# Two GRU recurrences on one core: recurrent products written several times, shorter input chunks, another order on VectorE

## The chip, the core and the metric

The kernel runs on one core of one Trainium2 chip. The metric is the time of one execution on the device, in microseconds. The core's engines run side by side and meet at semaphores: TensorE (PE in the rows; PEld is its weight load), VectorE (DVE), ScalarE (ACT), GpSimd (POOL) and SyncE (SP).

## The reference

Four layers are applied to an input of 8 images of 16 x 16 positions with 96 channels: a Fourier layer, a Toeplitz layer, and two GRU layers (L2 and L3). The GRU layers take most of the time. Each runs four GRUs over the 256 positions (two weight sets, each forward and reversed), and one step of a GRU is

```
def step(hprev, gxt):
    gh = hprev @ whh.T + bhh
    r = jax.nn.sigmoid(gxt[:, :h] + gh[:, :h])
    z = jax.nn.sigmoid(gxt[:, h:2 * h] + gh[:, h:2 * h])
    n = jnp.tanh(gxt[:, 2 * h:] + r * gh[:, 2 * h:])
    hn = (1.0 - z) * n + z * hprev
    return (hn, hn)
```

with h = 96, a batch of 8 and gx the input's share, known for all steps beforehand. There are 256 such steps in a layer, one after the other, so 512 in the kernel.

## The kernel before

Each GRU layer has an input part (`gru_input`), the steps (`gru_steps`) and an output part (`gru_output`). The change is in `gru_steps` alone.

The four GRUs stand in two **groups** of two (g = 0 and 1; the two inside a group are j = 0 and 1, so a group works on 16 columns, PER). The groups don't depend on each other, and each engine takes them in turn, so that one group's products run while the other group's gates are computed.

To keep fp32 accuracy from fp16 products, the state is held as a sum of two fp16 parts, `h_hi` and `h_lo`, and each weight as two as well. For each step and group TensorE runs (L1123, in `add`) twelve products with h_hi (three gates, two GRUs, two weight parts), waits for h_lo, and runs six products with h_lo. Each has 8 columns. The gates come in the order candidate, reset, keep; after the last h_lo product of the reset gate `reset_summed` is raised, after the last of all `keep_summed`. Then come some **input products** (L1105): the input's share is not computed step by step but for a chunk of STEPS = 8 steps, 36 products of 64 columns for the next chunk, dealt out over the steps of the current one.

All sums stand in PSUM, in two banks a group and chunk parity: `early` (reset, and the candidate's two summands) and `late` (keep). A bank holds 512 columns, of which `early` uses 384 and `late` 128.

ScalarE, for each group: sigmoid of the reset sum (L1071), sigmoids of the keep sum for z and 1-z (L1073, L1074), tanh of the candidate (L1077). VectorE: `candidate`, a scan that makes r times the recurrent share plus the input share (L1022); `kept_part`, z times the old state (L1029); `new_state`, two scans that make the same new state, once rounded to fp16 as h_hi (L1037, first, since TensorE waits for it) and once in fp32 into `states` (L1039); `rest`, which subtracts h_hi from the state and gives h_lo (L1045). `candidate` waits for the reset gate; `rest` waits for the fp32 state; `new_state` waits for tanh and for `kept_part`.

Each engine works strictly in the order written. On VectorE this is

```
for q in range(SEQ):
    candidate(0, q)
    rest(1, q - 1)
    kept_part(0, q)
    new_state(0, q)
    rest(0, q)
    candidate(1, q)
    kept_part(1, q)
    new_state(1, q)
```

Of the kernel before, what the change touches and what calls it, by code (L numbers as in the profile page):

```python
# [25 lines left out]
F32 = mybir.dt.float32  # L26
# [4 lines left out]
P = 128  # L31
BATCH, SIDE, C = 8, 16, 96
# [28 lines left out]
GRUS = ("f_%s_fw", "b_%s_rv", "f_%s_rv", "b_%s_fw")  # L61
GATES = 3

STEPS = 8
CHUNK_COUNT = SEQ // STEPS
GROUPS = 2

AFTER_0 = 0.7
PER = 2 * BATCH


def flat(ap):

    return ap.rearrange("p a b -> p (a b)")
# [893 lines left out]
def gru_steps(nc, layer, weights, forward, backward, states):  # L968
# [3 lines left out]
    with ExitStack() as ctx:  # L972
# [9 lines left out]

        h_hi = pairs("h_hi", [C + 1, 2, PER, 2], F16)
        h_lo = pairs("h_lo", [C, 2, PER], F16)
        early = [[ctx.enter_context(nc.psum_tensor(f"{layer}s_early{g}{p}", [P, 4, PER, STEPS], F32)) for p in range(2)] for g in range(GROUPS)]
        late = [[ctx.enter_context(nc.psum_tensor(f"{layer}s_late{g}{p}", [P, 4, PER, STEPS], F32)) for p in range(2)] for g in range(GROUPS)]
        reset_sum = lambda g, p: early[g][p][:, 0]
        cand_sum = lambda g, p: early[g][p][:, 1:3].rearrange("p a c s -> p (a c) s").rearrange("p (c k) s -> p c k s", k=2)
        keep_sum = lambda g, p: late[g][p][:, 0]
        warm = sb("warm", [C, 1])  # L990
        prepared = sem("prepared")

# [5 lines left out]
        with nc.Block() as block:  # L998

            @block.vector  # L1000
            def _(e):

                e.memset(warm[:], 0.0).then_inc(prepared, 1)
                for g in range(GROUPS):
                    for buffer in (reset[g], renew[g], terms[g], h_lo[g]):
                        e.memset(buffer[:], 0.0).then_inc(prepared, 1)
                    e.memset(states[g][:, 0], 0.0).then_inc(prepared, 1)
                    e.memset(h_hi[g][0:C], 0.0).then_inc(prepared, 1)
                    e.memset(h_hi[g][C:C + 1], 1.0).then_inc(prepared, 1)
                e.wait_ge(prepared, PREPARED)  # L1010

                for s, n in ((updated[1], 2), (hi_ready[0], 1), (hi_ready[1], 1), (lo_ready[0], 1)):
                    e.sem_inc(s, n)

                BEFORE = (0, 2)

                def candidate(g, q):

                    p, s = q // STEPS % 2, q % STEPS
                    x = q % 2  # L1020
                    e.wait_ge(activated[g], 3 * q + 1)
                    e.tensor_tensor_scan(flat(cand[g][:, x]), flat(reset[g][:, x]), flat(cand_sum(g, p)[0:C, :, :, s]), 0.0,  # L1022
                                         ALU.mult, ALU.add).then_inc(cand_ready[g], 1)

                def kept_part(g, q):

                    x = q % 2
                    e.wait_ge(activated[g], 3 * q + 2)
                    e.tensor_tensor(terms[g][:, x, :, 1], keep[g][:, x], states[g][:, q, :, 1], ALU.mult)\  # L1029
                        .then_inc(updated[g], 1)  # L1030

                def new_state(g, q):

                    x = q % 2
                    e.wait_ge(activated[g], 3 * q + 3)
                    e.wait_ge(updated[g], 2 * q + 1 + BEFORE[g])
                    e.tensor_tensor_scan(flat(h_hi[g][0:C, x]), flat(renew[g][:, x]), flat(terms[g][:, x]), 0.0,  # L1037
                                         ALU.mult, ALU.add).then_inc(hi_ready[g], 1)
                    e.tensor_tensor_scan(flat(states[g][:, q + 1]), flat(renew[g][:, x]), flat(terms[g][:, x]), 0.0,  # L1039
                                         ALU.mult, ALU.add).then_inc(updated[g], 1)  # L1040

                def rest(g, q):

                    e.wait_ge(updated[g], 2 * q + 2 + BEFORE[g])
                    e.tensor_tensor(h_lo[g][:, q % 2], states[g][:, q + 1, :, 1], h_hi[g][0:C, q % 2, :, 1],  # L1045
                                    ALU.subtract).then_inc(lo_ready[g], 1)

                for q in range(SEQ):
                    candidate(0, q)
                    rest(1, q - 1)  # L1050
                    kept_part(0, q)
                    new_state(0, q)
                    rest(0, q)
                    candidate(1, q)
                    kept_part(1, q)
                    new_state(1, q)
                e.wait_ge(updated[1], 2 * SEQ + BEFORE[1])

            @block.scalar
            def _(e):  # L1060
# [4 lines left out]
                for q in range(SEQ):  # L1065
                    p, s = q // STEPS % 2, q % STEPS
                    x = q % 2
# [11 lines left out]
            @block.tensor  # L1079
            def _(e):  # L1080
                def inputs(p, chunk):

                    out = []
                    cols = slice(chunk * STEPS, (chunk + 1) * STEPS)
                    for gru in range(len(GRUS)):
                        g, j = divmod(gru, 2)
                        source = forward if gru < 2 else backward
                        mine = slice(j * BATCH, (j + 1) * BATCH)

                        def share(dst, gate, first):  # L1090
                            for wp, xp in ((0, 0), (1, 0), (0, 1)):
                                rows = C if xp else C + 1
                                lhsT = weights.input[0:rows, wp, GATES * gru + gate, :]
                                rhs = source[0:rows, xp, :, cols]
                                out.append((dst, lhsT, rhs, first and (wp, xp) == (0, 0)))


                        share(reset_sum(g, p)[:, mine], 0, j == 0)
                        share(cand_sum(g, p)[:, mine, 1], 2, False)
                        share(keep_sum(g, p)[:, mine], 1, j == 0)  # L1100
                    return out

                def run(product):
                    dst, lhsT, rhs, start = product
                    return e.matmul(dst, lhsT, rhs, start=start, stop=False, skip_group_check=True)  # L1105

                for product in inputs(0, 0):
                    run(product)
                e.wait_ge(prepared, PREPARED)
                for q in range(SEQ):  # L1110
                    p, s = q // STEPS % 2, q % STEPS
                    x = (q + 1) % 2
                    if s == 0:
                        following = q // STEPS + 1
                        ahead = inputs(1 - p, following) if following < CHUNK_COUNT else []
                        sent = 0
                    for g in range(GROUPS):
                        def add(gate, wp, xp, j):
                            mine = slice(j * BATCH, (j + 1) * BATCH)
                            rows = C if xp else C + 1  # L1120
                            rhs = h_lo[g][:, x, mine] if xp else h_hi[g][:, x, mine, 1]
                            dst = (reset_sum(g, p)[:, mine, s], keep_sum(g, p)[:, mine, s], cand_sum(g, p)[:, mine, 0, s])[gate]
                            return e.matmul(dst, weights.hidden[0:rows, wp, GATES * (2 * g + j) + gate, :], rhs,  # L1123
                                            start=False, stop=False, skip_group_check=True)


                        e.wait_ge(hi_ready[g], q + 1)
                        for gate in (2, 0, 1):
                            for j in range(2):
                                add(gate, 0, 0, j)  # L1130
                                add(gate, 1, 0, j)

                        e.wait_ge(lo_ready[g], q + 1)
                        for gate in (2, 0, 1):
                            for j in range(2):
                                last = add(gate, 0, 1, j)
                            if gate == 0:
                                last.then_inc(reset_summed[g], 1)
                        last.then_inc(keep_summed[g], 1)

                        due = round((s + (AFTER_0 if g == 0 else 1)) * len(ahead) / STEPS)
                        for product in ahead[sent:due]:
                            run(product)
                        sent = due
# [196 lines left out]
```

## Time and profile before

| | |
|---|---|
| median of 3 runs | 1243.77 us (1241.73 to 1247.79) |
| profiled execution, its own time | 1242.83 us |
| its span in the trace | 1241.1 us |
| TensorE busy | 1066.6 us, 86% |
| VectorE busy | 931.8 us, 75% |
| ScalarE busy | 665.8 us, 54% |
| mean granted TensorE clock | 0.585 of full speed |

The two recurrences run from about 298 to 733 us and from about 780 to 1216 us. Busy shares are averages over stages with different limits; a recurrence is bound by a chain of small operations that wait for each other, so it has to be read from the timeline of single steps: start times, one after the other, on all engines. TensorE's clock has two levels, 1.2 and 2.4 GHz; the rows give it as a share of 2.4 GHz.

### The profile page before, as it was taken

The page shows a single profiled execution, that of the slowest core. Times are in us where ns is not written, and L with a number is a line of the kernel's source. Part 1 is how long each engine was busy: PE and PEld are TensorE (multiplying, and loading weights), DVE is VectorE, ACT ScalarE, POOL GpSimd, SP SyncE. Part 2 cuts the span into 40 slices and gives each one's busy share as a digit, 9 for nine tenths or more (in the row PEclk, how much of TensorE's full clock was granted, in tenths as well). Part 3 has the DMA queues.
Part 4 walks back from the last instruction along what each step waited for, and adds up shares of the span by engine and source line. Part 5 has one row for each costly group of instructions (what it writes and reads, how often), then busy time and mean ns, then how long its engine had stood idle before and what let it go on. Part 6 is the DMA issues. An engine that isn't in the chain of part 4 may idle for free. (4 is left out here: it accounts for less than half of the span.)

```text
span 1241.1 us, 56119 instructions
## 1 busy us (share of the span) xinstructions
PE 1066.6 (86%) x22390; PEld 814.7 (66%) x22390; DVE 931.8 (75%) x5703; ACT 665.8 (54%) x4269; POOL 116.7 (9%) x96
## 2 busy tenths in 40 slices
PE   3778799768999999999999968899999999999985
PEld 2555254355777777777777755677777777777775
DVE  3553799984777777777777785677777777777776
ACT  4224620007666666666666654666666666666663
POOL 1001389910000000000000001000000000000000
PEclk9587899957555555555555557655555555555555
DMA  4000500000000000000000000000000000000000
GB/s 117 2 8 5 129 1 1 1 5 2 4 4 3 4 4 4 3 4 4 4 4 3 4 2 5 3 4 4 4 4 3 4 4 4 3 4 4 4 3 27
DMA packets 8225, 12.63 MB, mean 10 GB/s; under 512 B 5745, under 2 KB 7121, under 8 KB 7674
## 3 DMA queue, kind: packets, MB, share of 16 engines
q1 hardware_dynamic: 7962, 9.05, 2.9%
q8 instruction: 175, 2.87, 1.0%
q14 instruction: 88, 0.72, 0.2%
HBM read 8.26 MB, written 0.79 MB: 7 GB/s over the span
## 5 line engine op out<-in xcount | busy, mean ns | idle before, releaser
L1123 PE MATMUL L3s_early<-L3s_h_hi,L_w_hidden 97*128 97x8 f16 x4096 | 195.3, 177 | 38.7 <-DVE L3s_h_hi L1037 5.2
L1123 PE MATMUL L2s_early<-L2s_h_hi,L_w_hidden 97*128 97x8 f16 x4096 | 195.3, 177 | 37.8 <-DVE L2s_h_hi L1037 5.4
L1123 PEld LDWEIGHTS L3s_early<-L3s_h_hi,L_w_hidden 97*128 97x128 f16 x4096 | 148.8, 105 | 111.2 <-DVE L3s_h_hi L1037 81.8
L1123 PEld LDWEIGHTS L2s_early<-L2s_h_hi,L_w_hidden 97*128 97x128 f16 x4096 | 148.8, 105 | 110.0 <-DVE L2s_h_hi L1037 77.4
L1037 DVE TENSOR_TENSOR_SCAN L3s_h_hi<-L3s_renew,L3s_terms 96x32 f16<-96x32 f32 x512 | 113.2, 221 | 84.8 <-ACT L3s_terms L1077 59.1
L1037 DVE TENSOR_TENSOR_SCAN L2s_h_hi<-L2s_renew,L2s_terms 96x32 f16<-96x32 f32 x512 | 113.2, 221 | 83.8 <-ACT L2s_terms L1077 57.4
L1077 ACT ACTIVATE L3s_terms<-L3s_cand 96x16 f32<-96x16 f32 x512 | 111.5, 218 | 106.0 <-DVE L3s_cand L1022 105.9
L1077 ACT ACTIVATE L2s_terms<-L2s_cand 96x16 f32<-96x16 f32 x512 | 111.5, 218 | 104.7 <-DVE L2s_cand L1022 104.6
L1123 PE MATMUL L3s_early<-L3s_h_lo,L_w_hidden 96*128 96x8 f16 x2048 | 131.0, 174 | 0.2 <-DVE L3s_h_lo L1045 0.2
L1123 PE MATMUL L2s_early<-L2s_h_lo,L_w_hidden 96*128 96x8 f16 x2048 | 130.9, 174 | 0.2 <-DVE L2s_h_lo L1045 0.2
L1123 PE MATMUL L2s_late<-L2s_h_hi,L_w_hidden 97*128 97x8 f16 x2048 | 130.0, 174 | 0.0
L1123 PE MATMUL L3s_late<-L3s_h_hi,L_w_hidden 97*128 97x8 f16 x2048 | 130.0, 174 | 0.0
L1071 ACT ACTIVATE L2s_reset<-L2s_early 96x16 f32<-96x16 f32 x512 | 93.0, 182 | 55.1 <-PE L2s_early L1123 55.1
L1071 ACT ACTIVATE L3s_reset<-L3s_early 96x16 f32<-96x16 f32 x512 | 93.0, 182 | 54.7 <-PE L3s_early L1123 54.7
L693 DVE SCALAR_TENSOR_TENSOR l_acc<-l_v,coef,l_acc 96x384 f32<-96x384 f32 (+11 forms) x88 | 103.6, 1241 | 0.4
L1022 DVE TENSOR_TENSOR_SCAN L3s_cand<-L3s_reset,L3s_early 96x32 f32<-96x32 f32 x512 | 102.5, 200 | 1.2 <-ACT L3s_reset L1071 1.2
L1022 DVE TENSOR_TENSOR_SCAN L2s_cand<-L2s_reset,L2s_early 96x32 f32<-96x32 f32 x512 | 102.3, 200 | 1.2 <-ACT L2s_reset L1071 1.2
L1123 PE MATMUL L2s_late<-L2s_h_lo,L_w_hidden 96*128 96x8 f16 x1024 | 102.7, 174 | 0.0
L1123 PE MATMUL L3s_late<-L3s_h_lo,L_w_hidden 96*128 96x8 f16 x1024 | 102.7, 174 | 0.0
L1039 DVE TENSOR_TENSOR_SCAN L_states<-L2s_renew,L2s_terms 96x32 f32<-96x32 f32 x512 | 99.9, 195 | 0.0
L1039 DVE TENSOR_TENSOR_SCAN L_states<-L3s_renew,L3s_terms 96x32 f32<-96x32 f32 x512 | 99.9, 195 | 0.0
L1045 DVE TENSOR_TENSOR L2s_h_lo<-L_states,L2s_h_hi 96x16 f16<-96x16 f32 x512 | 87.9, 172 | 9.1
(243 smaller groups left out, 2477.7 us busy)
## 6 DMA issues: line engine op xcount, KB each, us to landing
L_wih_raw<-in_L_wih SPq DMA_DIRECT2D x2, 1152.0 KB, 11.0
l_w_raw<-in_L_w SPq DMA_DIRECT2D x1, 1296.0 KB
L_w_hidden_raw<-in_L_whh SPq DMA_DIRECT2D x2, 576.0 KB
stream<-in_x SPq DMA_DIRECT2D x2, 384.0 KB, 3.8
out<-stream SPq DMA_DIRECT2D x4, 192.0 KB, 2.1
l_idft<-in_idft SPq DMA_DIRECT2D x1, 400.0 KB
rpe_lw<-in_rpe_lw SPq DMA_DIRECT2D x1, 384.0 KB
l_dft<-in_dft SPq DMA_DIRECT2D x1, 288.0 KB, 2.9
```

Of the source, the lines that this page charges most:

```text
L693: e.scalar_tensor_tensor(out=row(to, acc), in0=row(of, v), scalar=coef[:, m, axis, at:at + 1], in1=row(to, acc), op0=ALU.mult, op1=ALU.add ...
L1022: e.tensor_tensor_scan(flat(cand[g][:, x]), flat(reset[g][:, x]), flat(cand_sum(g, p)[0:C, :, :, s]), 0.0, ALU.mult, ALU.add).then_inc(can ...
L1037: e.tensor_tensor_scan(flat(h_hi[g][0:C, x]), flat(renew[g][:, x]), flat(terms[g][:, x]), 0.0, ALU.mult, ALU.add).then_inc(hi_ready[g], 1)
L1039: e.tensor_tensor_scan(flat(states[g][:, q + 1]), flat(renew[g][:, x]), flat(terms[g][:, x]), 0.0, ALU.mult, ALU.add).then_inc(updated[g], 1)
L1045: e.tensor_tensor(h_lo[g][:, q % 2], states[g][:, q + 1, :, 1], h_hi[g][0:C, q % 2, :, 1], ALU.subtract).then_inc(lo_ready[g], 1)
L1071: e.activation(reset[g][:, x, :, 1], reset_sum(g, p)[0:C, :, s], ACT.Sigmoid).then_inc(activated[g], 1)
L1077: e.activation(terms[g][:, x, :, 0], cand[g][:, x, :, 1], ACT.Tanh).then_inc(activated[g], 1)
L1123: return e.matmul(dst, weights.hidden[0:rows, wp, GATES * (2 * g + j) + gate, :], rhs, start=False, stop=False, skip_group_check=True)
```

## The change

1. Each recurrent product is written to three places (reset) or four (candidate, keep) in one matmul: the same 8 columns of the state are read three or four times (a broadcast of the moving operand), and the output goes to the 8 columns that are read later and to 16 or 24 columns of the same bank that nobody reads. A recurrent matmul so has 24 or 32 columns instead of 8.
2. To make room for these, a chunk has 4 steps instead of 8: the banks are laid out as eight parts of 16 x 4 columns in place of four parts of 16 x 8. The input products become 36 of 32 columns for every 4 steps.
3. On VectorE the second group's candidate scan stands ahead of the first group's `rest`.

```
-STEPS = 8
+STEPS = 4
...
-        early = [[... psum_tensor(f"{layer}s_early{g}{p}", [P, 4, PER, STEPS], F32) ...
-        late = [[... psum_tensor(f"{layer}s_late{g}{p}", [P, 4, PER, STEPS], F32) ...
+        early = [[... psum_tensor(f"{layer}s_early{g}{p}", [P, 8, PER, STEPS], F32) ...
+        late = [[... psum_tensor(f"{layer}s_late{g}{p}", [P, 8, PER, STEPS], F32) ...
...
                     new_state(0, q)
+                    candidate(1, q)
                     rest(0, q)
-                    candidate(1, q)
                     kept_part(1, q)
...
-                            dst = (reset_sum(g, p)[:, mine, s], keep_sum(g, p)[:, mine, s], cand_sum(g, p)[:, mine, 0, s])[gate]
-                            return e.matmul(dst, weights.hidden[0:rows, wp, GATES * (2 * g + j) + gate, :], rhs,
+                            halves = early[g][p].rearrange("p a (c k) s -> p a c k s", k=2)
+                            spread = (early[g][p][:, 0:7:3, mine, s], late[g][p][:, 0:4, mine, s],
+                                      halves[:, (slice(1, 8, 2), slice(2, 6))[j], :, 0, s])[gate]
+                            copies = spread.shape[1]
+                            return e.matmul(spread, weights.hidden[0:rows, wp, GATES * (2 * g + j) + gate, :],
+                                            rhs.unsqueeze(1).to_broadcast([rows, copies, BATCH]),
```

On VectorE, in the middle of the first recurrence's steps, the digit behind a name being the group (behind `early` the group and the chunk's parity). Before:

```order
L1037 SCALAR_TENSOR_TENSOR L2s_h_hi0<-L2s_renew0,L2s_terms0 96x32
L1039 SCALAR_TENSOR_TENSOR L2_states0<-L2s_renew0,L2s_terms0 96x32
L1045 TENSOR_TENSOR L2s_h_lo0<-L2_states0,L2s_h_hi0 96x16
L1022 SCALAR_TENSOR_TENSOR L2s_cand1<-L2s_reset1,L2s_early10 96x32
L1029 TENSOR_TENSOR L2s_terms1<-L2s_keep1,L2_states1 96x16
L1037 SCALAR_TENSOR_TENSOR L2s_h_hi1<-L2s_renew1,L2s_terms1 96x32
L1039 SCALAR_TENSOR_TENSOR L2_states1<-L2s_renew1,L2s_terms1 96x32
L1022 SCALAR_TENSOR_TENSOR L2s_cand0<-L2s_reset0,L2s_early00 96x32
L1045 TENSOR_TENSOR L2s_h_lo1<-L2_states1,L2s_h_hi1 96x16
```

And after, where all lines of the file are one higher here:

```order
L1038 SCALAR_TENSOR_TENSOR L2s_h_hi0<-L2s_renew0,L2s_terms0 96x32
L1040 SCALAR_TENSOR_TENSOR L2_states0<-L2s_renew0,L2s_terms0 96x32
L1023 SCALAR_TENSOR_TENSOR L2s_cand1<-L2s_reset1,L2s_early10 96x32
L1046 TENSOR_TENSOR L2s_h_lo0<-L2_states0,L2s_h_hi0 96x16
L1030 TENSOR_TENSOR L2s_terms1<-L2s_keep1,L2_states1 96x16
L1038 SCALAR_TENSOR_TENSOR L2s_h_hi1<-L2s_renew1,L2s_terms1 96x32
L1040 SCALAR_TENSOR_TENSOR L2_states1<-L2s_renew1,L2s_terms1 96x32
L1023 SCALAR_TENSOR_TENSOR L2s_cand0<-L2s_reset0,L2s_early00 96x32
L1046 TENSOR_TENSOR L2s_h_lo1<-L2_states1,L2s_h_hi1 96x16
```

Group 0's h_lo has gone behind group 1's candidate scan, as group 1's h_lo stood behind group 0's already. On TensorE, for one group and the turn after it, before (the last figure is partitions x columns, `x8` the number of such matmuls in a row):

```order
L1123 MATMUL L2s_early<-L2s_h_hi,L_w_hidden 128x8 x8
L1123 MATMUL L2s_late<-L2s_h_hi,L_w_hidden 128x8 x4
L1123 MATMUL L2s_early<-L2s_h_lo,L_w_hidden 128x8 x4
L1123 MATMUL L2s_late<-L2s_h_lo,L_w_hidden 128x8 x2
L1105 MATMUL L2s_late<-L_backward,L_w_input 128x64
```

And after, where the recurrent products are at L1127 and the input products at L1106:

```order
L1127 MATMUL L2s_early<-L2s_h_hi,L_w_hidden 128x4x8 x2
L1127 MATMUL L2s_early<-L2s_h_hi,L_w_hidden 128x32 x2
L1127 MATMUL L2s_early<-L2s_h_hi,L_w_hidden 128x3x8 x4
L1127 MATMUL L2s_late<-L2s_h_hi,L_w_hidden 128x4x8 x4
L1127 MATMUL L2s_early<-L2s_h_lo,L_w_hidden 128x4x8
L1127 MATMUL L2s_early<-L2s_h_lo,L_w_hidden 128x32
L1127 MATMUL L2s_early<-L2s_h_lo,L_w_hidden 128x3x8 x2
L1127 MATMUL L2s_late<-L2s_h_lo,L_w_hidden 128x4x8 x2
L1106 MATMUL L2s_late<-L_backward,L_w_input 128x32 x3
```

The number and order of the recurrent products are the same, each is three or four times as wide; the input products of a turn are six behind group 0 and three behind group 1, of 32 columns.

## Rows read from the trace of the kernel before

**Rows 1.** The page: busy time, and the granted clock in 40 slices.

```profile
PE 1066.6 (86%) x22390; PEld 814.7 (66%) x22390; DVE 931.8 (75%) x5703; ACT 665.8 (54%) x4269; POOL 116.7 (9%) x96
...
PEclk9587899957555555555555557655555555555555
```

**Rows 2.** Groups of instructions from 784 to 1200 us: count, busy us, mean ns.

```profile
L1123 PE MATMUL L3s_late<-L3s_h_lo,L_w_hidden 96*128 96x8 f16 x978 | 98.1, 174 | 0.0
L1022 DVE TENSOR_TENSOR_SCAN L3s_cand<-L3s_reset,L3s_early 96x32 f32<-96x32 f32 x489 | 97.9, 200 | 0.0
```

**Rows 3.** Timeline of one step at 1.2 GHz: start us, us, engine, line.

```profile
784.33 0.32 PE L1105 MATMUL L3s_early<-L_forward,L_w_input 97*128 97x64 f16 x3
...
785.24 0.22 DVE L1037 TENSOR_TENSOR_SCAN L3s_h_hi<-L3s_renew,L3s_terms 96x32 f16<-96x32 f32 x1
...
785.41 0.18 ACT L1071 ACTIVATE L3s_reset<-L3s_early 96x16 f32<-96x16 f32 x1 [0.21 <-PE L3s_early L1123]
...
785.52 0.38 PE L1123 MATMUL L3s_early<-L3s_h_hi,L_w_hidden 97*128 97x8 f16 x8
...
785.61 0.17 DVE L1045 TENSOR_TENSOR L3s_h_lo<-L_states,L3s_h_hi 96x16 f16<-96x16 f32 x1
785.70 0.21 DVE L1022 TENSOR_TENSOR_SCAN L3s_cand<-L3s_reset,L3s_early 96x32 f32<-96x32 f32 x1
...
785.86 0.25 PE L1123 MATMUL L3s_early<-L3s_h_lo,L_w_hidden 96*128 96x8 f16 x4
...
785.95 0.22 ACT L1077 ACTIVATE L3s_terms<-L3s_cand 96x16 f32<-96x16 f32 x1 [0.20 <-DVE L3s_cand L1022]
...
786.15 0.18 ACT L1071 ACTIVATE L3s_reset<-L3s_early 96x16 f32<-96x16 f32 x1
786.19 0.22 DVE L1037 TENSOR_TENSOR_SCAN L3s_h_hi<-L3s_renew,L3s_terms 96x32 f16<-96x32 f32 x1 [0.22 <-ACT L3s_terms L1077]
...
786.34 0.20 DVE L1039 TENSOR_TENSOR_SCAN L_states<-L3s_renew,L3s_terms 96x32 f32<-96x32 f32 x1
786.45 0.19 DVE L1022 TENSOR_TENSOR_SCAN L3s_cand<-L3s_reset,L3s_early 96x32 f32<-96x32 f32 x1
...
786.67 0.22 ACT L1077 ACTIVATE L3s_terms<-L3s_cand 96x16 f32<-96x16 f32 x1 [0.20 <-DVE L3s_cand L1022]
...
786.93 0.22 DVE L1037 TENSOR_TENSOR_SCAN L3s_h_hi<-L3s_renew,L3s_terms 96x32 f16<-96x32 f32 x1
```

**Rows 4.** Timeline, the second recurrence's first steps.

```profile
781.15 0.18 ACT L1071 ACTIVATE L3s_reset<-L3s_early 96x16 f32<-96x16 f32 x1 [0.53 <-PE L3s_early L1123]
...
781.36 0.22 DVE L1022 TENSOR_TENSOR_SCAN L3s_cand<-L3s_reset,L3s_early 96x32 f32<-96x32 f32 x1 [1.16 <-ACT L3s_reset L1071]
781.50 0.15 DVE L1045 TENSOR_TENSOR L3s_h_lo<-L_states,L3s_h_hi 96x16 f16<-96x16 f32 x1
...
781.70 0.26 PE L1123 MATMUL L3s_early<-L3s_h_lo,L_w_hidden 96*128 96x8 f16 x4 [0.21 <-DVE L3s_h_lo L1045]
...
782.00 0.18 ACT L1071 ACTIVATE L3s_reset<-L3s_early 96x16 f32<-96x16 f32 x1 [0.17 <-PE L3s_early L1123]
...
782.14 0.36 PE L1123 MATMUL L3s_early<-L3s_h_hi,L_w_hidden 97*128 97x8 f16 x8
...
783.83 0.38 PE L1123 MATMUL L3s_early<-L3s_h_hi,L_w_hidden 97*128 97x8 f16 x8
```

**Rows 5.** Stretches: length, TensorE's busy us, further engines' in the second, granted clock.

```profile
741.00:754.00 13.00, 13.00 (x63) 0.50 0.00 1
...
782.00:784.00 2.00, 1.70 (x49) 1.39 (x48) 1.61 (x13) 1.35 (x11) 0.00 (x0) 0.90 0.00 0
```

**Rows 6.** Groups from 400 to 700 us: single input products.

```profile
L1105 PE MATMUL L2s_late<-L_backward,L_w_input 96*128 96x64 f16 x44 | 9.4, 214 | 0.0
```

**Rows 7.** Timeline, the first recurrence's first step.

```profile
298.94 0.22 DVE L1022 TENSOR_TENSOR_SCAN L2s_cand<-L2s_reset,L2s_early 96x32 f32<-96x32 f32 x1 [1.16 <-ACT L2s_reset L1071]
...
299.59 0.18 ACT L1071 ACTIVATE L2s_reset<-L2s_early 96x16 f32<-96x16 f32 x1 [0.18 <-PE L2s_early L1123]
```

More of the change, by code:

```diff
@@ L984, in gru_steps @@
         h_lo = pairs("h_lo", [C, 2, PER], F16)
-        early = [[ctx.enter_context(nc.psum_tensor(f"{layer}s_early{g}{p}", [P, 4, PER, STEPS], F32)) for p in range(2)] for g in range(GROUPS)]
-        late = [[ctx.enter_context(nc.psum_tensor(f"{layer}s_late{g}{p}", [P, 4, PER, STEPS], F32)) for p in range(2)] for g in range(GROUPS)]
+        early = [[ctx.enter_context(nc.psum_tensor(f"{layer}s_early{g}{p}", [P, 8, PER, STEPS], F32)) for p in range(2)] for g in range(GROUPS)]
+        late = [[ctx.enter_context(nc.psum_tensor(f"{layer}s_late{g}{p}", [P, 8, PER, STEPS], F32)) for p in range(2)] for g in range(GROUPS)]
         reset_sum = lambda g, p: early[g][p][:, 0]
```

## Prediction

> **What bounds the kernel now.** The page first [rows 1]: the span is 1241.1 us, TensorE (PE) is busy 86% of it, VectorE (DVE) 75%, and its costliest lines are the recurrent products and the small operations of the GRU step. Then the clock line of the slices [rows 1]: in nearly all slices of the two recurrences TensorE is granted half its speed, 1.2 GHz. The invitation is to blame the clock. The table of groups [rows 2] gives the size of the stage: 489 candidate scans in 416 us, two to a step, are 1.70 us a step, and 512 steps in all are about 871 us of the span.
>
> What ends each step is read from the timeline of one step at 1.2 GHz [rows 3], by start times. The first group's h_hi scan (L1037) starts at 785.24, the state scan (L1039) right behind it (0.15 us, as at 786.34); the difference h_lo (L1045), which needs that scan's result, at 785.61; only then the second group's candidate scan (L1022) at 785.70, although its reset gate (L1071) had started at 785.41 and ended at 785.59; its tanh at 785.95; its h_hi scan at 786.19; its state scan at 786.34; the first group's candidate scan at 786.45; the tanh at 786.67; and the first group's next h_hi scan at 786.93. That is a closed ring of VectorE and ScalarE (ACT) alone: 0.37+0.09+0.25+0.24+0.15+0.11+0.22+0.26 = 1.69 us, the whole period. No matmul is in it. TensorE's part runs beside it with a little room. The path of one group alone is h_hi scan to h_hi product 785.24 to 785.52 (0.28), product to reset gate 785.52 to 786.15 (0.63), reset gate to candidate scan 0.21 where nothing stands between (781.15 to 781.36 [rows 4]), to tanh 0.22, to scan 0.26: 1.60 us.
>
> The same step at 2.4 GHz stands in the first steps of the second recurrence. The first group's h_hi products start at 782.14 and 783.83 [rows 4], again 1.69 us apart, though the clock is still 0.90 on average from 782 to 784 [rows 5], so 1.00 for all but the last 0.4 us. So **a fast TensorE by itself buys nothing in today's order**: the ring does not contain it.
>
> **The change, part by part.**
>
> *Wider products.* Each step's 36 recurrent matmuls stream 24 columns (reset) or 32 (candidate, keep) instead of 8. Two prices: the spacing, and the last column's arrival. Spacing: twelve h_hi matmuls at 1.2 GHz take 785.52 to 785.86, 28 ns each [rows 3]; three of 64 columns take 0.32 us (784.33) where one takes 0.21 [rows 3, 6], so 55 ns each. 32 columns lie halfway in columns, but 64 columns at 1.2 GHz are 53 ns, so 32 are 27 ns and fit under the 28 ns that a small product takes anyway. I take zero; the other end, the 64-column price, adds 27 ns to each of three gaps ahead of the reset sum. Arrival: a product of 64 columns lasts 214 ns, of 8 columns 174 [rows 2, 6], 40 ns for 56 columns, so 16 more columns in the last reset product cost 11 ns. At 2.4 GHz I take half, 6 ns (an estimate from the two clock levels). The Trainium skill (TensorE: Matmul & The Clock Gate, Single matmul latency) prices columns at N/1.2 and N/2.4 ns, 13 and 7 ns here; the trace agrees within its modelled ends.
>
> *The clock.* What could be gained from it is small: the half ring below is 0.85 us at one level and 0.86 at the other. In the steps the h_hi and h_lo products start 0.34 us apart (785.52 and 785.86 [rows 3]), TensorE never rests long, and the clock is 0.50 all the same. Will it rise? TensorE was granted 1.2 GHz for the whole 13 us in which it ran 96-column fp32 products (L1217) back to back, busy 13.00 of 13.00 us [rows 5]; and it fell from 2.4 to 1.2 GHz some 3 us after the second recurrence began its steps [rows 5], though the products run there as densely as they ever do. The high slices lie where products of hundreds of columns run densely [rows 1]. The widened step is 36 products of 24 or 32 columns and 9 of 32, with waits between; that is nearer to the rows where it stayed low or fell. I take 1.2 GHz. The Trainium skill (same page, Why this matters for your kernels) says that the clock stays high as long as TensorE has no long idle gaps between bursts; by that rule it would be high in the steps already and the wider products could change nothing. The trace does not follow the rule here.
>
> *Chunks of four.* The input products become 36 of 32 columns per four steps: nine a step instead of 4.5, 9 x 28 ns against 4.5 x 55: nothing. They stand behind the reset and keep products in TensorE's queue. First group: six each step, 0.17 us, second: three. A group's turn on TensorE is then 0.34 us for the h_hi products (785.52 to 785.86), six h_lo products, 0.17, and six input products, 0.17: 0.68 us of the 0.87 that a half step has, so 0.19 us are idle and cover them. If h_lo comes 0.1 us late that cover still holds; without it each 0.1 us would be 0.1 on the half step. The first chunk's products lie ahead of step 0, beside the memsets.
>
> *The second candidate scan ahead of the first group's low half.* This breaks the present ring: state scan to candidate scan directly, 0.11 instead of 0.23+0.09, so that ring would be 1.48 us (786.34 to 786.45 for the direct link [rows 3]). But it closes another. The order on VectorE is then candidate(0), h_lo(1), ..., candidate(1), h_lo(0): each group's h_lo stands behind the other group's candidate scan, the h_lo products wait for it, the reset gate waits for these, and the group's own candidate scan waits for the reset gate. Half of the ring is: candidate scan, h_lo, h_lo product, reset gate, next candidate scan. It is in the trace twice where the scan had waited, as it will in the new order, at the first step of each recurrence: 781.36 to 781.50 (0.14), to the product at 781.70 (0.20), to the reset gate at 782.00 (0.30), and from gate to scan 781.15 to 781.36 (0.21) [rows 4]: **0.85 us** at 2.4 GHz. In the other recurrence scan to reset gate is 298.94 to 299.59 (0.65) [rows 7], with 0.21 **0.86 us**; I take that for 1.2 GHz. Both halves must pass within one step, so the period is 2 x 0.86 = 1.72 us before the columns. Add 11 ns to each: 2 x 0.871 = 1.742 us. Today's order has only one such half in a ring; the other passes through tanh and the scans, 1.60 us in all.
>
> **The sum.** At 1.2 GHz: 1.742 - 1.69 = +0.052 us a step, x 512 = +26.6 us. The profiled execution took 1242.83 us (0.9 below the median of 1243.77, which I leave aside), so **1269 us**. Everything outside the recurrences stays: a higher clock in the steps is not counted on for the output products, which come after a pause of several us.
>
> **Rivals.**
>
> *The clock rises (all or much of the time).* For it: more than three times the columns, and the fp32 products' columns may not compare with fp16's. Then each half is 0.85+0.006, the period 1.712, +0.022 x 512 = +11: **1254 us**. Alternating levels lie between. Chance 0.22.
>
> *Faster.* The two sampled halves are first steps. If the new order lets VectorE and TensorE run as smoothly as now, each link takes its shortest row: VectorE to its next operation 0.11 (786.34 to 786.45), h_lo to product 0.20, product to reset gate 0.29 (785.86 to 786.15), gate to scan 0.21 [rows 3, 4], 0.81 us, so 1.62 to 1.64, with columns at 2.4 GHz 1.65: -0.04 x 512 = -20, **1222 us**. The deciding point is a half of 0.845 us; under it the reorder gains, and at 0.80 the single group's path (1.60) takes over at 1242.8 - 46 = 1197. Against it: in both samples the product waits for h_lo, which adds the weight load to the path. Chance 0.27.
>
> *Wide patterns cost as 64 columns.* Three gaps ahead of the reset sum cost 27 ns more each in each half: 2 x 0.08 x 512 = +83 on the forecast, 1350. A quarter of that is 1290. The arithmetic above speaks against it. Chance 0.07.
>
> *Nothing moves*: the loss by the new ring and the gain by its shorter links meet. 1238 to 1249. Chance 0.10, in part beside the edges of the two others.
>
> **How the numbers follow.** Forecast 0.34 with its own range 1258 to 1282; risen clock 0.22; faster 0.27; dear columns 0.07; nothing 0.10. The range goes to 1222 below (half of the faster case is left out) and 1284 above. Changes under 0.5%, or 6 us, cannot be told from none by a measurement. Faster by over 0.5% (under 1237.6) is the faster case, 0.27; within 0.5% the last case and the risen clock's lower edge, 0.14; slower the rest, 0.59.
>
> **What would show it.** The step length by the starts of one group's h_hi products: 1.74 us, or 1.71 or 1.65. VectorE's candidate scan should follow the state scan after a wait on the reset gate and no more on h_lo, and TensorE should wait on h_lo (L1046) at each group of each step, which it does not now. The slices' clock digit shows 5 if the wide products do not raise it. The prediction is wrong if TensorE shows no wait for h_lo, if the clock is 9 and the reset gate follows the first h_lo product by clearly less than 0.30 us, or if small wide products stand more than 30 ns apart.

## The result and the profile after

The changed kernel takes 1271.05 us (median of 4 runs, 1268.57 to 1275.6) against 1245.78 us for the kernel before beside it; the ratio is 1.021, with a 95% interval of 1.0167 to 1.0253. It is slower by some 25 us between the medians, 26 by the ratio. The forecast was 1269 us, so size and sign came out; two of the terms behind it did not: TensorE's clock, and the price of the wider products.

The page of the changed kernel: busy time, the granted clock in 40 slices, and the groups of the first recurrence's reset gates and candidate scans (the last field of a group is the idle time before its instructions and what ended it).

```profile
PE 1147.1 (91%) x24694; PEld 917.5 (72%) x24694; DVE 969.5 (77%) x5703; ACT 671.9 (53%) x4269; POOL 116.7 (9%) x96
...
PEclk9587899868999999999999977899999999999996
...
L1072 ACT ACTIVATE L2s_reset<-L2s_early 96x16 f32<-96x16 f32 x512 | 92.7, 181 | 98.9 <-PE L2s_early L1127 98.9
...
L1023 DVE TENSOR_TENSOR_SCAN L2s_cand<-L2s_reset,L2s_early 96x32 f32<-96x32 f32 x512 | 110.8, 216 | 19.6 <-ACT L2s_reset L1072 2.1
```

The clock line is full of nines where the kernel before had fives [rows 1]. The reset gates wait 98.9 us for the product sums; the page of the kernel before has this for the same gates:

```profile
L1071 ACT ACTIVATE L2s_reset<-L2s_early 96x16 f32<-96x16 f32 x512 | 93.0, 182 | 55.1 <-PE L2s_early L1123 55.1
```

So TensorE runs at twice the clock, and the gates wait 1.8 times as long for its sums. The timeline of one step of the changed kernel says why (start us, us, engine, line):

```profile
700.49 0.22 DVE L1023 TENSOR_TENSOR_SCAN L2s_cand<-L2s_reset,L2s_early 96x32 f32<-96x32 f32 x1
...
700.63 0.15 DVE L1046 TENSOR_TENSOR L2s_h_lo<-L_states,L2s_h_hi 96x16 f16<-96x16 f32 x1
...
700.83 0.28 PE L1127 MATMUL L2s_early<-L2s_h_lo,L_w_hidden 96*128 96x32 f16 x4
...
701.15 0.18 ACT L1072 ACTIVATE L2s_reset<-L2s_early 96x16 f32<-96x16 f32 x1 [0.19 <-PE L2s_early L1127]
...
701.37 0.22 DVE L1023 TENSOR_TENSOR_SCAN L2s_cand<-L2s_reset,L2s_early 96x32 f32<-96x32 f32 x1
...
701.50 0.15 DVE L1046 TENSOR_TENSOR L2s_h_lo<-L_states,L2s_h_hi 96x16 f16<-96x16 f32 x1
...
701.70 0.28 PE L1127 MATMUL L2s_early<-L2s_h_lo,L_w_hidden 96*128 96x32 f16 x4
...
702.02 0.18 ACT L1072 ACTIVATE L2s_reset<-L2s_early 96x16 f32<-96x16 f32 x1 [0.19 <-PE L2s_early L1127]
...
702.23 0.22 DVE L1023 TENSOR_TENSOR_SCAN L2s_cand<-L2s_reset,L2s_early 96x32 f32<-96x32 f32 x1
```

This is the ring of the prediction, closed twice in a step: candidate scan to h_lo 0.14 or 0.13, to the h_lo product 0.20, to the reset gate 0.32, to the next candidate scan 0.21 or 0.22, together 0.87 us; 700.49 to 702.23 is 1.74 us. The prediction had 0.14, 0.20, 0.31+0.011, 0.21, and 1.742. All four links are the predicted ones, and the third has nearly the predicted length, but at 2.4 GHz and not at 1.2.

A longer stretch gives the step more finely. It shows length, then busy us and number of instructions for PE, PEld, DVE, ACT and POOL, then the granted clock. A step has ten VectorE operations, so 400 us divided by a tenth of VectorE's number is the step: 1.750 us in the changed kernel (x2286). In the kernel before it is 1.698 us (x2356), which is 0.052 us less:

```profile
320.00:720.00 400.00, 366.89 (x9536) 299.60 (x9536) 314.35 (x2356) 253.54 (x1887) 0.00 (x0) 0.50 0.01 4
```

What the change does at 1.2 GHz is in the changed kernel's own trace. Four of its stretches, the long one first:

```profile
320.00:720.00 400.00, 390.96 (x10292) 335.16 (x10293) 322.10 (x2286) 248.68 (x1830) 0.00 (x0) 1.00 0.02 4
302.00:304.00 2.00, 2.00 (x50) 2.00 (x47) 1.41 (x10) 1.16 (x10) 0.00 (x0) 0.50 0.01 4
304.00:306.00 2.00, 2.00 (x53) 2.00 (x50) 1.41 (x10) 1.17 (x10) 0.00 (x0) 0.58 0.04 8
306.00:308.00 2.00, 1.88 (x55) 1.57 (x53) 1.59 (x12) 1.29 (x11) 0.00 (x0) 1.00 0.01 4
```

The timeline of a step at the low clock:

```profile
300.44 0.37 PE L1127 MATMUL L2s_early<-L2s_h_lo,L_w_hidden 96*128 96x32 f16 x4
...
300.60 0.22 DVE L1038 TENSOR_TENSOR_SCAN L2s_h_hi<-L2s_renew,L2s_terms 96x32 f16<-96x32 f32 x1
...
300.85 0.18 ACT L1072 ACTIVATE L2s_reset<-L2s_early 96x16 f32<-96x16 f32 x1 [0.28 <-PE L2s_early L1127]
...
302.60 0.22 DVE L1038 TENSOR_TENSOR_SCAN L2s_h_hi<-L2s_renew,L2s_terms 96x32 f16<-96x32 f32 x1
```

The steps begin at about 298 us with the clock high; it falls within the first microsecond and then stays low for some 7 us. In that time TensorE is busy without a gap, a step takes 2.00 us (the same group's h_hi scan at 300.60 and 302.60), and h_lo product to reset gate is 0.41 us. Between 304 and 306 the clock rises and stays. Had it stayed low, 512 steps of 2.00 us would by this estimate have cost 0.30 x 512 = 154 us, not 26.

### The profile page after: what moved, and what is told of

Same layout as the page of the kernel before. It is cut to its first block and busy times, and to the rows that moved or that the text cites. A ratio compares the mean times of both kernels' runs of the same rounds, so it can differ in the third digit from the quotient of the medians.

```text
span 1266.8 us, 60727 instructions
## 1 busy us (share of the span) xinstructions
PE 1147.1 (91%) x24694; PEld 917.5 (72%) x24694; DVE 969.5 (77%) x5703; ACT 671.9 (53%) x4269; POOL 116.7 (9%) x96
## 5 line engine op out<-in xcount | busy, mean ns | idle before, releaser
L1127 PE MATMUL L3s_early<-L3s_h_hi,L_w_hidden 97*128 97x32 f16 (+1 forms) x4096 | 199.9, 190 | 11.5 <-DVE L3s_h_hi L1038 2.9
L1127 PE MATMUL L2s_early<-L2s_h_hi,L_w_hidden 97*128 97x32 f16 (+1 forms) x4096 | 199.9, 190 | 10.8 <-DVE L2s_h_hi L1038 2.2
L1127 PEld LDWEIGHTS L3s_early<-L3s_h_hi,L_w_hidden 97*128 97x128 f16 x4096 | 145.4, 98 | 50.8 <-DVE L3s_h_hi L1038 5.2
L1127 PEld LDWEIGHTS L2s_early<-L2s_h_hi,L_w_hidden 97*128 97x128 f16 x4096 | 145.4, 97 | 50.6 <-DVE L2s_h_hi L1038 4.5
L1072 ACT ACTIVATE L2s_reset<-L2s_early 96x16 f32<-96x16 f32 x512 | 92.7, 181 | 98.9 <-PE L2s_early L1127 98.9
L1127 PE MATMUL L2s_early<-L2s_h_lo,L_w_hidden 96*128 96x32 f16 (+1 forms) x2048 | 143.9, 192 | 0.2
L1127 PE MATMUL L3s_early<-L3s_h_lo,L_w_hidden 96*128 96x32 f16 (+1 forms) x2048 | 143.9, 192 | 0.0
L1127 PE MATMUL L2s_late<-L2s_h_hi,L_w_hidden 97*128 97x32 f16 x2048 | 142.5, 193 | 0.0
L1127 PE MATMUL L3s_late<-L3s_h_hi,L_w_hidden 97*128 97x32 f16 x2048 | 142.4, 193 | 0.0
L1023 DVE TENSOR_TENSOR_SCAN L2s_cand<-L2s_reset,L2s_early 96x32 f32<-96x32 f32 x512 | 110.8, 216 | 19.6 <-ACT L2s_reset L1072 2.1
L1023 DVE TENSOR_TENSOR_SCAN L3s_cand<-L3s_reset,L3s_early 96x32 f32<-96x32 f32 x512 | 110.8, 216 | 19.5 <-ACT L3s_reset L1072 1.9
L1127 PE MATMUL L3s_late<-L3s_h_lo,L_w_hidden 96*128 96x32 f16 x1024 | 112.1, 192 | 0.0
L1127 PE MATMUL L2s_late<-L2s_h_lo,L_w_hidden 96*128 96x32 f16 x1024 | 112.1, 192 | 0.0
L1127 PEld LDWEIGHTS L2s_early<-L2s_h_lo,L_w_hidden 96*128 96x128 f16 x2048 | 88.8, 98 | 22.4 <-DVE L2s_h_lo L1046 0.4
L1127 PEld LDWEIGHTS L3s_early<-L3s_h_lo,L_w_hidden 96*128 96x128 f16 x2048 | 88.8, 98 | 22.0
L1040 DVE TENSOR_TENSOR_SCAN L_states<-L3s_renew,L3s_terms 96x32 f32<-96x32 f32 x512 | 100.0, 195 | 0.0
```

The source lines that it names most:

```text
L1072: e.activation(reset[g][:, x, :, 1], reset_sum(g, p)[0:C, :, s], ACT.Sigmoid).then_inc(activated[g], 1)
L1127: return e.matmul(spread, weights.hidden[0:rows, wp, GATES * (2 * g + j) + gate, :], rhs.unsqueeze(1).to_broadcast([rows, copies, BATCH]), ...
```

## The experiments

Theory 1 is the ring: the new order on VectorE makes each group's reset gate depend on the other's candidate scan, twice in a step. Theory 2 puts the loss on the wide products, whatever the order.

**The order alone**, on the kernel before:

```
                     new_state(0, q)
+                    candidate(1, q)
                     rest(0, q)
-                    candidate(1, q)
```

> The kernel before with nothing changed but VectorE's order: the second group's candidate scan ahead of the first group's h_lo. Products of 8 columns, chunks of 8. Theory 1 (the ring: candidate scan, h_lo, h_lo product, reset gate, and the same through the other group): a step is 2 x (0.14+0.20+0.31+0.21) = 1.72 us at 1.2 GHz, +0.02 to 0.03 us on each of 512 steps, 1254 to 1260 us, and the reset gate waits for TensorE in every turn. Theory 2 (the loss comes from the wide products, whatever the order): no loss, 1241 to 1248 us. Clock 0.50 by both.

Measured: 1265.45 us, ratio 1.0165 (1.0145 to 1.0186). The timeline:

```profile
700.65 0.22 DVE L1022 TENSOR_TENSOR_SCAN L2s_cand<-L2s_reset,L2s_early 96x32 f32<-96x32 f32 x1
...
700.78 0.15 DVE L1045 TENSOR_TENSOR L2s_h_lo<-L_states,L2s_h_hi 96x16 f16<-96x16 f32 x1
...
700.99 0.28 PE L1123 MATMUL L2s_early<-L2s_h_lo,L_w_hidden 96*128 96x8 f16 x4
...
701.30 0.18 ACT L1071 ACTIVATE L2s_reset<-L2s_early 96x16 f32<-96x16 f32 x1 [0.18 <-PE L2s_early L1123]
...
701.52 0.22 DVE L1022 TENSOR_TENSOR_SCAN L2s_cand<-L2s_reset,L2s_early 96x32 f32<-96x32 f32 x1
```

A stretch of 400 us of the same kernel:

```profile
320.00:720.00 400.00, 390.96 (x9301) 326.86 (x9299) 323.02 (x2298) 250.53 (x1839) 0.00 (x0) 0.50 0.02 4
```

The ring is there with narrow products at 1.2 GHz: 0.13+0.21+0.31+0.22 = 0.87 us. Moving one call up by one place carries about 20 of the 26 us. The time is 5 us above the upper end of what was expected: a step is 1.741 us (x2298), so a half is 0.870 us instead of 0.86.

**The other parts alone**: the changed kernel with the old order.

```
                     new_state(0, q)
-                    candidate(1, q)
                     rest(0, q)
+                    candidate(1, q)
```

> The changed kernel with VectorE's old order: wide products, chunks of four. Theory 1: the ring of VectorE and ScalarE binds again, 1.69 to 1.70 us a step, whatever the clock, 1241 to 1250 us. Theory 2: the loss stays, 1262 to 1272 us. The clock should be above 0.9 in the steps, as in the changed kernel, since the same columns are streamed.

Measured: 1244.52 us, ratio 1.0009 (0.9993 to 1.0026). The timeline:

```profile
700.47 0.22 DVE L1038 TENSOR_TENSOR_SCAN L2s_h_hi<-L2s_renew,L2s_terms 96x32 f16<-96x32 f32 x1
...
700.84 0.17 DVE L1046 TENSOR_TENSOR L2s_h_lo<-L_states,L2s_h_hi 96x16 f16<-96x16 f32 x1
...
700.93 0.21 DVE L1023 TENSOR_TENSOR_SCAN L2s_cand<-L2s_reset,L2s_early 96x32 f32<-96x32 f32 x1
...
702.16 0.22 DVE L1038 TENSOR_TENSOR_SCAN L2s_h_hi<-L2s_renew,L2s_terms 96x32 f16<-96x32 f32 x1
```

A stretch of 400 us of the same kernel:

```profile
320.00:720.00 400.00, 364.78 (x10604) 319.95 (x10601) 314.27 (x2355) 256.01 (x1885) 0.00 (x0) 1.00 0.02 4
```

The clock is 1.00 for 400 us and the step is as long as at 0.50: 1.69 us from scan to scan (700.47 to 702.16), 1.699 over the stretch (x2355), with the same first links 0.37 and 0.09 as in the ring of [rows 3]. Theory 2 falls, and the prediction's reading of [rows 4], that a fast TensorE buys nothing in the old order, holds over a whole kernel.

**Chunks of four alone** (STEPS = 4 and banks of eight parts, products of 8 columns, old order).

> The kernel before with chunks of four steps and the wider banks' layout alone: products of 8 columns, old order on VectorE. The prediction took this part at nothing: 1241 to 1248 us, clock 0.50, 1.69 us a step. If twice as many input products crowd TensorE, the h_hi products of the next turn start later and the step grows with them.

Measured: 1247.9 us, ratio 1.0024 (1.0006 to 1.0041). In the profiled execution the steps are as long as before: over the same 400 us VectorE ran x2357 instructions against x2356. By the interval a cost of 1 to 5 us is possible; where it would lie was not found, and the kernel before this one, which has the same chunks, shows none that is clear of noise (0.9993 to 1.0026).

**Which wide products cost, at which clock.** Of the wide products, first the h_lo ones made narrow again, then the h_hi ones:

```
+                            if xp:        # in the second kernel: if not xp:
+                                dst = (reset_sum(g, p)[:, mine, s], keep_sum(g, p)[:, mine, s], cand_sum(g, p)[:, mine, 0, s])[gate]
+                                return e.matmul(dst, weights.hidden[0:rows, wp, GATES * (2 * g + j) + gate, :], rhs,
+                                                start=False, stop=False, skip_group_check=True)
```

> The changed kernel, but the six h_lo products have 8 columns as before; only the twelve h_hi products are written three or four times. Theory 1 with the columns as the cost of the last link: if the clock stays high, h_lo product to reset gate falls from 0.32 to 0.30 us, the step from 1.74 to 1.70 us, 1246 to 1254 us. If the fewer columns let the clock fall, 0.31 us and 1.72 us, 1254 to 1260 us. If the columns do not matter and something else makes the link 0.32, the time stays at 1271.

> The changed kernel, but only the six h_lo products are written three or four times, the twelve h_hi products have 8 columns. In the kernel with only h_hi wide, the wide products stood 47 ns apart at 1.2 GHz, though input products of 32 columns stand 26 ns apart there. Two causes are open: h_hi is read with a stride of two elements, h_lo is read densely; and the outputs are scattered in both. If the stride of the moving operand is the cause, the wide h_lo products stand some 27 ns apart and the time is 1262 to 1275 us; if it is the output's or the broadcast's pattern, they stand some 47 ns apart, the reset gate comes 0.06 us later in each half and the time is 1320 to 1335 us. Clock near 0.50 by both, the columns being fewer than in the kernel whose clock stayed low.

Measured: 1345.86 us with only h_hi wide (ratio 1.0815, 1.0796 to 1.0834) and 1357.15 us with only h_lo wide (1.0900, 1.0872 to 1.0927). Both expectations were missed, the first widely (it named times from 1246 to 1271 us), the second by 22 us (1320 to 1335). The timeline of the first kernel:

```profile
700.74 0.55 PE L1131 MATMUL L2s_early<-L2s_h_hi,L_w_hidden 97*128 97x32 f16 x8
...
701.11 0.39 PE L1131 MATMUL L2s_late<-L2s_h_hi,L_w_hidden 97*128 97x32 f16 x4
```

A stretch of 400 us of the same kernel:

```profile
320.00:720.00 400.00, 398.38 (x9478) 392.09 (x9475) 296.93 (x2107) 229.01 (x1685) 0.00 (x0) 0.50 0.02 4
```

The timeline of the second kernel:

```profile
700.94 0.37 PE L1131 MATMUL L2s_early<-L2s_h_lo,L_w_hidden 96*128 96x32 f16 x4
...
701.34 0.18 ACT L1072 ACTIVATE L2s_reset<-L2s_early 96x16 f32<-96x16 f32 x1 [0.28 <-PE L2s_early L1131]
```

The two groups of wide products of the second kernel with 32 columns each, first the candidate's, then the keep gate's (320 to 720 us; count, busy us, mean ns):

```profile
L1131 PE MATMUL L2s_early<-L2s_h_lo,L_w_hidden 96*128 96x32 f16 x832 | 119.5, 237 | 10.9
L1131 PE MATMUL L2s_late<-L2s_h_lo,L_w_hidden 96*128 96x32 f16 x832 | 117.2, 235 | 0.0
```

The clock stayed at 1.2 GHz in both kernels, and there eight wide products take 0.37 us from first to next, 46 ns each, where narrow ones take 28 [rows 3]. The loss is not the same in the two. With h_lo wide, product to reset gate is 0.40 us and the half ring 0.96 us: the ring has grown. With h_hi wide, TensorE is full (398.38 of 400 us) and sets the pace itself. Since h_lo is read densely and h_hi with a stride, the stride of the input is not the cause.

**Two copies instead of three or four** (16 columns).

> The changed kernel with each recurrent product written twice instead of three or four times: 16 columns. If the clock stays at 1.2 GHz and a wide product costs by its columns, the products stand 28 to 35 ns apart: 1265 to 1300 us. If the clock rises, the link from h_lo product to reset gate is between the 0.30 us of 8 columns and the 0.32 of 24: 1255 to 1271 us.

Measured: 1279.04 us, ratio 1.0273 (1.0248 to 1.0298), in the range expected for a low clock. The timeline, and a stretch of 400 us:

```profile
701.08 0.29 PE L1127 MATMUL L2s_early<-L2s_h_lo,L_w_hidden 96*128 96x16 f16 x4
...
701.40 0.18 ACT L1072 ACTIVATE L2s_reset<-L2s_early 96x16 f32<-96x16 f32 x1 [0.20 <-PE L2s_early L1127]
```

```profile
320.00:720.00 400.00, 394.91 (x10195) 341.98 (x10192) 319.04 (x2265) 246.11 (x1812) 0.00 (x0) 0.50 0.02 4
```

Here the link is 0.32 us at 1.2 GHz: slower than one copy (0.31) and, over the kernel, 8 us slower than four copies with the clock they bring.

**What makes a wide product dear.** The recurrent products are narrow again (chunks of four, new order). Behind each turn stand four additional products of 32 columns, one form in each of four steps. In words instead of code:

```
L1150: out spare[:, 4, 0:8, :] as 32 in a row;  in forward[0:C, 0, 0, 0:32]
L1152: out spare[:, 4:8, 0:8, s], 16 bytes apart;  in the same
L1154: out 32 in a row;  in forward[0:C, 0, 0, 0:8] read four times
L1156: out 32 in a row;  in forward[0:C, 0, 0, 0:64:2]
```

> A look at what makes a wide recurrent product dear at 1.2 GHz. Products of 8 columns, chunks of four, new order; behind each turn four further products of 32 columns that the result does not need, one form in each of four steps in turn: dense input and dense output (L1150); dense input and output scattered as the candidate's copies are, 16 bytes apart (L1152); the same 8 columns read four times, dense output (L1154); input read with a stride of two, dense output (L1156). If scattered output is the cause, L1152 alone stands some 50 ns apart at 1.2 GHz and the rest 27; if the broadcast is, L1154 alone; if the stride of the input, L1156 alone. Time about 1265 to 1290.

Measured: 1260 us, a single run, used here only for its trace. The timeline:

```profile
500.38 0.37 PE L1152 MATMUL L2s_early<-L_forward,L_w_hidden 96*128 96x32 f16 x4
...
501.33 0.27 PE L1154 MATMUL L2s_early<-L_forward,L_w_hidden 96*128 96x32 f16 x4
...
503.06 0.27 PE L1156 MATMUL L2s_early<-L_forward,L_w_hidden 96*128 96x32 f16 x4
...
504.80 0.27 PE L1150 MATMUL L2s_early<-L_forward,L_w_hidden 96*128 96x32 f16 x4
```

Groups of this trace from 320 to 720 us (count, busy us, mean ns, idle), the last one of input products:

```profile
L1152 PE MATMUL L2s_early<-L_forward,L_w_hidden 96*128 96x32 f16 x456 | 42.7, 235 | 0.0
...
L1154 PE MATMUL L2s_early<-L_forward,L_w_hidden 96*128 96x32 f16 x464 | 31.0, 188 | 0.0
...
L1105 PE MATMUL L2s_early<-L_backward,L_w_input 97*128 97x32 f16 x464 | 34.1, 188 | 0.0
```

One form alone is dear: the output scattered 16 bytes apart. Its product lasts 235 ns against 188, so 47 ns more for 32 columns, and (0.37-0.235)/3 = 45 ns stand between two against 27. Neither the broadcast nor the stride of the input costs anything. The input products last 188 ns as well, although half of those in `early` (the candidate's) write runs of four neighbouring columns with gaps between: it is the single columns that are dear. One thing in the expectation is not so: in the changed kernel the reset and keep copies stand 16 bytes apart, but the candidate's 32. Both are dear, as the two groups of the kernel with only h_lo wide show (235 and 237 ns).

**The clock with narrow recurrent products.** To see what 2.4 GHz alone gives in the new order, additional products of 256 columns behind each turn (chunks of four, recurrent products of 8 columns): one dense, two dense, one scattered. The first:

```
+                            e.matmul(early[g][1 - p][:, 4:8].rearrange("p a c s -> p (a c s)"), weights.hidden[0:C, 0, 0, :],
+                                     forward[0:C, 0, 0, :], start=False, stop=False, skip_group_check=True)
```

> Recurrent products of 8 columns, chunks of four, VectorE's new order, and one further product of 256 columns behind each turn's input products, into columns that nobody reads. It adds work that the result does not need. If it lifts the clock as the wide products do, this is the new ring at 2.4 GHz without wide products in it: 2 x (0.14+0.20+0.30+0.21) = 1.70 us a step, 1246 to 1254 us, against 1265 at 1.2 GHz: the price of the wide products in the changed kernel would then be some 20 us and the clock's gain some 12. If the clock stays low, the 256 columns (0.21 us) push the next turn's h_hi products back by 0 to 0.05 us, which the h_lo wait covers: 1265 us.

> As the kernel with one filler, but two products of 256 columns behind each turn, work that the result does not need. The single filler left the clock at 1.2 GHz. At 1.2 GHz two take 0.43 us, a turn of TensorE is then 0.50+0.12+0.43 = 1.05 us, more than the 0.87 of the ring, so the step would be 2.1 us and TensorE never idle: if the clock follows that, it rises, a turn is 0.46+0.12+0.22 = 0.80 us, and the ring binds at 2.4 GHz with narrow products: 2 x 0.85 = 1.70 us, 1246 to 1256 us. If it does not rise: about 1440 us. If the time stays at 1265 with the clock high, the clock gives nothing even where TensorE is in the ring.

> As the kernel with one filler of 256 columns (clock 1.2 GHz, 1266 us), but the filler's output is scattered, 16 bytes from column to column, like the wide products'. The filler is work that the result does not need. At 1.2 GHz it should take 0.43 us instead of 0.21, so TensorE is full for 1.05 us a turn. If scattered products lift the clock where dense ones of the same length did not, it rises, the turn is 0.46+0.12+0.22 = 0.80 us and the ring binds with narrow products at 2.4 GHz: 2 x 0.85 = 1.70 us a step, 1246 to 1256 us. If the clock stays low: about 1420 us, as with two dense fillers.

Measured: 1265.97 us (ratio 1.0161, 1.0133 to 1.0190), 1422.02 us (1.1418) and 1421.99 us (1.1408). The stretch of 400 us with one dense product, with two dense ones, then with one scattered:

```profile
320.00:720.00 400.00, 399.62 (x10803) 369.81 (x10799) 323.57 (x2298) 249.80 (x1838) 0.00 (x0) 0.50 0.02 4
```

```profile
320.00:720.00 400.00, 400.00 (x9553) 350.92 (x9551) 274.70 (x1950) 211.77 (x1558) 0.00 (x0) 0.50 0.01 4
```

```profile
320.00:720.00 400.00, 400.00 (x9161) 324.00 (x9159) 274.37 (x1948) 211.87 (x1559) 0.00 (x0) 0.50 0.01 4
```

In the last two TensorE is busy in 400.00 of 400.00 us and is granted 1.2 GHz throughout. No kernel with narrow products ran at 2.4 GHz in the new order, so the gain of the clock there stays unmeasured. The one dense product shows two things: it costs nothing (ratio 1.0161 against 1.0165 for the order alone, and the same step, x2298), so TensorE has 0.2 us of room in each turn, as the prediction worked out, and what binds is h_lo.

**h_lo on GpSimd**, to open both rings: the kernel before with `rest` moved off VectorE.

```
-                    rest(1, q - 1)
...
-                    rest(0, q)
...
+            @block.gpsimd
+            def _(e):
+                e.wait_ge(prepared, PREPARED)
+                for q in range(SEQ):
+                    for g in range(GROUPS):
+                        e.wait_ge(updated[g], 2 * q + 2 + 2 * g)
+                        e.tensor_tensor(h_lo[g][:, q % 2], states[g][:, q + 1, :, 1], h_hi[g][0:C, q % 2, :, 1],
+                                        ALU.subtract).then_inc(lo_ready[g], 1)
```

> The kernel before (8 columns, chunks of 8), with both h_lo subtractions moved from VectorE to GpSimd, so that neither ring closes on VectorE. Theory 1: what is left is one group's own path, 1.60 us a step if GpSimd gives h_lo within 0.6 us of the h_hi scan: 1197 to 1215 us. Every 0.1 us that GpSimd's operation is later than that adds 0.1 us to a step: with an operation of 0.4 us the step would be about 1.8 us and the time about 1300. Theory 2 says nothing of it.

> The kernel whose h_lo comes from GpSimd, with chunks of four and the scattered filler behind each turn (not needed by the result). There the ring is one group's own: state scan, GpSimd, h_lo product, reset gate, candidate scan, tanh, 1.71 us at 1.2 GHz. If the clock rises, the link from h_lo product to reset gate falls from 0.31 to 0.30 us and the step to 1.69 to 1.70: 1243 to 1250 us, against 1252. If it stays low, TensorE's turn of 1.05 us binds: about 1420 us.

Measured: 1252.05 us (ratio 1.0066, 1.0049 to 1.0083); with the scattered filler 1423.81 us (1.1431), since the clock did not rise there either. The timeline of the first:

```profile
700.49 0.22 DVE L1037 TENSOR_TENSOR_SCAN L2s_h_hi<-L2s_renew,L2s_terms 96x32 f16<-96x32 f32 x1 [0.17 <-ACT L2s_terms L1079]
...
700.63 0.20 DVE L1039 TENSOR_TENSOR_SCAN L_states<-L2s_renew,L2s_terms 96x32 f32<-96x32 f32 x1
...
700.90 0.22 POOL L1058 TENSOR_TENSOR L2s_h_lo<-L_states,L2s_h_hi 96x16 f16<-96x16 f32 x1 [0.61 <-DVE L_states L1039]
...
701.18 0.27 PE L1125 MATMUL L2s_early<-L2s_h_lo,L_w_hidden 96*128 96x8 f16 x4
```

The expected 1197 to 1215 us were missed. They needed h_lo within 0.6 us of the h_hi scan; GpSimd starts 0.27 us after the state scan's start and the h_lo product stands 0.55 us behind that start, 0.69 behind the h_hi scan's. The lone group's path is so 1.71 us, not 1.60: opening both rings closed a third that is as long. None of the versions beats the kernel before.

## Why the prediction was right, and where it was not

**What bounds the kernel, and the ring of the new order: right and shown.** The new order alone gives 1.0165, everything else without it 1.0009.

**The ring's length: nearly right, a little too short.** 0.86 us at 1.2 GHz was predicted for narrow products from the first steps of the trace; 0.870 measured over 400 us. The hundredth counts 1024 times: the order was priced at +0.03 us a step (15 us) and measured at +0.043 (22 us by the steps, about 20 by the times; the step before was 1.698 us, not 1.69).

**The clock: wrong.** I took 1.2 GHz, with a chance of 0.22 for the rise. It is 1.00 in all but some 7 us near the start of each recurrence. The step that failed is the comparison with 96-column fp32 products and with the fall at the start of the steps: neither decides what the widened products do. The runs don't give a rule for it either: one or two additional products that fill TensorE to 400 of 400 us leave it low, 36 wide ones lift it, 24 narrow and 12 wide ones or the reverse don't, and 36 of 16 columns don't. What raises it stays open.

**The price of the columns: wrong at the low clock, and a little short at the high one.** "Spacing: zero" was read off products whose output is dense in PSUM. The copies' output is scattered, and then 24 or 32 columns take some 46 ns at 1.2 GHz, not 28. The prediction had named products more than 30 ns apart as a sign that it is wrong, and by that sign it was, in the stretch with the low clock. The rival that gave them the price of 64 columns (55 ns, 1350 us) came nearer to what happened there. That the two kernels with a part of the products wide took 1346 and 1357 us is no confirmation of its sum, which was for all 36; with all 36 a step took 2.00 us at that clock, near 1400 us in all by the estimate above.

At 2.4 GHz the scattered products are nearly back to the price of dense ones. In the changed kernel, from 320 to 720 us, they last 192 ns and input products of 32 columns 179, 13 ns apart where it is 47 at 1.2 GHz:

```profile
L1127 PE MATMUL L2s_late<-L2s_h_hi,L_w_hidden 97*128 97x32 f16 x1828 | 126.5, 192 | 0.0
...
L1106 PE MATMUL L2s_late<-L_backward,L_w_input 97*128 97x32 f16 x228 | 23.5, 179 | 0.0
```

h_lo product to reset gate is 0.32 us there, where I had 0.306 for a high clock and 0.321 for the low one. That the missing 0.014 comes from the outputs' layout is likely but not shown: no kernel of this order ran narrow products at 2.4 GHz.

**How much of the match is luck.** The two errors, low clock and cheap columns, met at 0.32: that the time was 1271 and not 1254 or 1400 is in that part luck. The parts of the sum were off too, in opposite directions. The order cost 0.043 us a step instead of 0.03; the rest, the wide products at their high clock with the chunks of four, cost 1.750 - 1.741 = 0.009 instead of 0.022. Together they are the 0.052 us that was forecast. In time that is about 20 us and about 6 us; the second is the difference of two ratios whose intervals overlap (1.0145 to 1.0186 and 1.0167 to 1.0253), so its size is uncertain.

**Chunks of four: taken at nothing, measured 0.06 to 0.41%** with a step of unchanged length. The predicted cover of 0.19 us in each of TensorE's turns is borne out by the dense product of 256 columns, which fits in.

**The rival "faster"** needed a half of under 0.845 us. It asked VectorE and TensorE to run as in the old stream. In the new ring the scan and the h_lo product both start after a wait: scan to h_lo is 0.13 to 0.14, not 0.11, and h_lo product to reset gate is 0.31 with narrow products after a wait, 0.29 without [rows 3].

The Trainium skill (TensorE: Matmul & The Clock Gate, Why this matters for your kernels) has the clock high as long as TensorE has no long idle gaps. The traces do not agree: the stretches with 400.00 of 400.00 us busy at 0.50 contradict that as a sufficient condition.

## What to carry to other kernels

Before reordering an in-order queue, follow the moved instruction's consumer until it comes back to the queue: here an h_lo moved by one place closed a ring through the other group, and two halves of 0.87 us took the place of one ring of 1.70. A faster clock on an engine that isn't in the ring was worth nothing here (ratio 1.0009 at clock 1.00 for the old order). And price a wider matmul by its output's layout, not by its columns alone.

## What the hardware showed that was not expected

- A matmul of 32 columns whose fp32 outputs stand 16 bytes apart in PSUM lasts 235 ns against 188 with dense outputs, and follows its like after some 45 ns instead of 27, at 1.2 GHz. At 2.4 GHz the difference in length is 13 ns. Reading the same 8 columns four times, or reading with a stride of two, cost nothing.
- TensorE was granted 1.2 GHz over 400 us in which it was busy all the time (two dense products of 256 columns or a scattered one in each turn), and 2.4 GHz in the changed kernel over 400 us in which it was busy for 390.96.
- Writing each product three or four times raised the clock, from 0.585 to 0.93 over the kernel, and bought nothing; twice did not raise it.
- GpSimd's subtraction of 96x16 takes 0.22 us against VectorE's 0.15 to 0.17, and its result reaches TensorE 0.55 us after the start of the scan that it waits for.
